# Position product of the first 32 tiles one edge step earlier, into the bank of their logits; ScalarE leaves out steps that do not exist and makes 22 one-hots before its last eviction

## The reference, cut to what matters

```python
agg = segment_sum(x[src], dst); neigh = agg / max(deg, 1)           # 106250 edges
h = x @ W_self + b_self + neigh @ W_neigh
h = prelu(layernorm(h) * gamma + beta) + x ; x1 = x + h              # x is layer-normed on the way in
x2 = layernorm(x1)
logits = x2 @ gate_weight.T ; top_vals, top_idx = top_k(logits, 2)
h = silu(x2 @ w1[e].T) for the picked experts; mean of h over each expert's tokens
y_mean[e] = h_mean[e] @ w2[e].T ; out = x1 + softmax(top_vals) . y_mean[top_idx]
```

## Time and profile before

| | us |
|---|---|
| median of 3 runs | 1636.46 (1634.24 to 1638.45) |
| span of the profiled execution | 1988.1 |
| of it, stretch of the edge steps (about 200 to 1618) | 1418 |
| of it, from 1618 to the end | 370 |
| TensorE, VectorE, GpSimd, ScalarE busy | 1311.0, 1077.1, 967.4, 892.4 |

### The profile page before, as it was taken

The page is one execution under the profiler, slowest core; times in us unless marked ns, Lnnn a source line. Parts: engine busy times, 40 slices in busy tenths (PEclk is TensorE's granted clock), DMA queues, the critical chain, the costliest instruction groups (busy, mean ns, idle before and its releaser), DMA issues.

```text
span 1988.1 us, 36507 instructions
## 1 busy us (share of the span) xinstructions
PE 1311.0 (66%) x7645; PEld 658.9 (33%) x7646; DVE 1077.1 (54%) x2604; ACT 892.4 (45%) x1939; POOL 967.4 (49%) x1237
## 2 busy tenths in 40 slices
PE   5999788995545555455545445455666643999996
PEld 3454344442212222222222222123333322677641
DVE  6663146554545535655655665453453666666626
ACT  3454444445333333333333333233444468888701
POOL 5321656565555556555555655555554511555500
PEclk9999899998778767776777777677778775999986
DMA  6452676766666766676667676665655643666466
GB/s 200 138 163 96 191 222 211 214 207 205 209 200 202 191 192 206 190 232 216 204 214 232 213 220 210 197 183 166 189 172 160 180 172 104 194 201 199 150 242 258
DMA packets 140571, 384.91 MB, mean 194 GB/s; under 512 B 22286, under 2 KB 22416, under 8 KB 140452
## 3 DMA queue, kind: packets, MB, share of 16 engines
q0 software_dynamic: 76416, 250.05, 43.4%
q1 hardware_dynamic: 62392, 130.43, 18.6%
q10 hardware_dynamic: 1644, 3.10, 0.4%
HBM read 323.78 MB, written 59.72 MB: 193 GB/s over the span
## 4 chain that ended last, share of the span: by engine, by line
PE 36%; POOL 22%; issue 19%; DMA 9%; another core or an unknown queue 3%; ACT 3%; DVE 3%; POOLq 3%; DVEq 0%; ACTq 0%; SPq 0%
POOL work L630 22%; PE ps L969 13%; DMA work<-table,work 8%; PE ps L868 8%; PE ps L1062 5%; PE ps L1073 2%; PE ps L1064 2%; POOLq L625 2%; PE ps L1103 1%; ACT slots L780 1%; PE ps L1125 1%; ACT wparts L770 1%; DMA work<-in_x 1%; PE ps L914 1%
## 5 line engine op out<-in xcount | busy, mean ns | idle before, releaser
L630 POOL DMA_INDIRECT work<-table,work x832 | 790.7, 950 | 641.0 <-PE ps L972 263.6
L969 PE MATMUL ps<-work 128*128 x2056 | 667.2, 474 | 544.5 <-DMA work<-table,work 421.2
L969 PEld LDWEIGHTS ps<-work 128*128 128x128 f16 x2056 | 228.7, 113 | 862.1 <-issue 758.1
L723 ACT ACTIVATE work<-work,ones 128x512 f16<-128x512 f16 x259 | 185.4, 716 | 538.0 <-remote 348.7
L717 ACT ACTIVATE work<-iota_row,work 128x128 f16<-128x128 f32 x1040 | 331.3, 390 | 31.6 <-ACT work L723 18.8
L1328 DVE TENSOR_SCALAR inv<-ps 128x1 f32 (+2 forms) x49 | 7.7, 158 | 583.6 <-remote 293.4
L868 PE MATMUL ps<-wparts,slots 128*128 128x512 f16 x1176 | 276.0, 386 | 17.8 <-DVE slots L1246 11.7
L646 POOL DMA_INDIRECT slots<-x_d,betab x114 | 108.0, 947 | 167.0 <-PE ps L1073 85.3
L868 PEld LDWEIGHTS ps<-wparts,slots 128*128 128x128 f16 x1176 | 112.8, 99 | 142.1 <-DVE slots L1246 14.2
L1062 PE MATMUL ps<-work,wparts 128*128 x456 | 155.7, 382 | 3.5 <-ACT wparts L812 2.1
L812 ACT COPY wparts<-ps 128x1024 f16<-128x1024 f16 x114 | 115.3, 1012 | 42.6 <-PE ps L1073 30.1
(11 more groups left out here) (272 smaller groups left out, 1574.0 us busy)
## 6 DMA issues: line engine op xcount, KB each, us to landing
work<-in_x SPq DMA_DIRECT2D x96, 256.0 KB, 2.8
work<-in_w_t SPq DMA_DIRECT2D x48, 512.0 KB, 11.2
work<-table,work POOLq DMA_INDIRECT x832
table<-work SPq DMA_DIRECT2D x48, 256.0 KB, 2.0
x_d<-work SPq DMA_DIRECT2D x48, 256.0 KB
x_d<-slots SPq DMA_DIRECT2D x48, 256.0 KB
out_x<-slots SPq DMA_DIRECT2D x48, 256.0 KB
slots<-x_d SPq DMA_DIRECT2D x41, 256.0 KB
```

The source lines that it names most:

```text
L630: pool.indirect_dma_start(out=gath[:, g % GRING, w, :], out_offset=None, in_=table[:, :], in_offset=bass.IndirectOffsetOnAxis(ap=idx_all[: ...
L723: act.activation(hot[:, slot, :, :], away[:, slot % 2, :, :], ACT.Relu, bias=ones[:, 0:1], scale=-1.0).then_inc(c_hot, 1)
L969: pe.matmul(ps[:, ds(bank, 1), :], hot[:, s, w, :], gath_row[:, ds(at + (2 * w + half) * D, D)].unsqueeze(1), start=False, stop=True, skip ...
```

## The change

1. TensorE: place(0) moves from behind step 255's gate to behind step 254's, and writes bank 6 (`POS_AT`), whose logits of tiles 0 to 31 route(0) has read. Its wait for `d_xt` is dropped.
2. ScalarE: in the late bodies the distances of steps past 256 and the one-hots of steps past 256 are left out (3 x 4 and 2 instructions, with their waits); SyncE's counts fall by 3 and 2.
3. ScalarE: 22 of the 48 pairs, in place of 16, stand before `take_turned(48)`.

```diff
-LOW_FIRST = 16
+LOW_FIRST = 22
-POS_AT = (5, 0)
+POS_AT = (6, 0)
...
-            sp.wait_ge(c_away, STEPS + 3)
-            sp.wait_ge(c_hot, STEPS + 2)
+            sp.wait_ge(c_away, STEPS)
+            sp.wait_ge(c_hot, STEPS)
...
-                    act.wait_ge(c_hot, k + 2)
-                    distance(k + 3, (s + 3) % 2)
-                    one_hots(k + 2, (s + 2) % HOTS)
+                    if not late or k + 3 < STEPS:
+                        act.wait_ge(c_hot, k + 2)
+                        distance(k + 3, (s + 3) % 2)
+                    if not late or k + 2 < STEPS:
+                        one_hots(k + 2, (s + 2) % HOTS)
...
-                    if late and k == STEPS - 2:
-                        pe.wait_ge(d_xt, k - LATE)
+                    if late and k == STEPS - 3:
                         place(0)
```

## The result

The changed kernel took 1630.74 us, median of 8 runs (1629.05 to 1632.73), beside 1634.70 of before on the same chip, also of 8. The ratio is 0.9973 with a 95% interval of 0.9964 to 0.9983: 2.8 to 5.9 us less. One of the 87 timed runs of the kernel before in this study took 2882.5 us and is left out of all ratios and means.

What follows compares the result with a forecast made beforehand. ScalarE's low one-hots were taken as the bound, VectorE 0.2 us behind. Savings of 1.79, 0.82 and 1.31 less 0.1 gave 3.8 us, 4.2 at timed pace; 4.0 taken: 1636.46 to 1632.5 us, range 1629.8 to 1636.5.

Steps and rivals of the forecast that it cites:

- Part 1: ScalarE, ahead of the first low one-hot: leaving out work for steps 258 and 259 saves 1.79 us on the path.
- its remark on 16 pairs: ScalarE before the copy of tile 48: 16 pairs first would leave it idle about 3.1 us there.
- Part 2: TensorE around step 256: place(0) one step earlier, without its wait, ends that step 0.82 us earlier; 1.2 at timed pace.
- the pace: Edge stage in the timed runs: an estimated 4.15 us a step, making the saving 1.2 us instead of 0.82.
- Part 3: ScalarE before the copy of tile 48: 22 pairs first remove its 1.31 us idle time; gate(48) just fits.
- the prediction's own signs: Wrong if gate(48) comes after VectorE asks, route(0) isn't done at place(0), or the list product's end moves without the gather.
- The sum: End of the list product: 3.8 us earlier by the profiled execution, 4.2 by the timed pace; 4.0 taken.
- T: Experiments' theory: VectorE isn't held at rows_to(0) in timed runs; skip and 22 pairs help only together, until VectorE is last.
- Full clock in step 256: TensorE's step 256 may stay at 2.4 GHz, giving 1.45 us more: -5.3, 1631.2 us; chance 0.22.
- VectorE as the bound: List product: if step 256 doesn't move, VectorE still ends at 1672.24, giving -3.0, 1633.5 us; chance 0.15.
- Hidden: Expert stage: another wait, w1's load or an instruction block, holds it, so the time stays 1636.5 us; chance 0.08.
- a stall of ScalarE: Among ScalarE's 22 pairs: a 5.7 us stall ahead of the copy of tile 48 gives 1638.2 us; chance 0.10.

Runs made afterwards that it cites:

- the second trace of before: The kernel before, unchanged, profiled once more for a trace at the pace of the timed runs; one run, 1636.18 us, span 1634.4.
- the run with 1.27: The changed kernel with place(0) back behind step 255, in bank 6 and without its wait; 1630.74 us, ratio 0.9975; VectorE idled 1.27 for place(0).

## Why the prediction came out as it did

**The bound and where the gain arrives: right.** The list product was what moved, ScalarE last before and VectorE a hair behind (0.2 us in both traces of before), and afterwards the last block waits for VectorE. The end of the list product carries through: from there to the end of the span lie 310.4 us before and 310.5 after.

**Part 1, 1.79 on ScalarE: the size right, its place on the path not by itself.** The pairs start 1.8 earlier once the turn of tile 47 takes as long (G + 21.61 against 19.83); the first trace shows 1.4, the turn having taken 1.01 instead of 0.61. Alone it buys nothing, as the run with the skip alone shows: it is worth something only because the 22 pairs take it up. The prediction knew this (its remark on 16 pairs), though it wrote "on the path".

**Part 2, place(0): the step that failed.** The prediction took -0.82 from the profiled execution and -1.2 by the timed pace for VectorE, TensorE's turn and ScalarE. Measured, gnn(48) starts at G + 18.15 before and G + 18.18 after: nothing. The failing term is the pace. I took 4.15 us for a step, a mean over all 257. TensorE's steps in the second trace of before:

```profile
1220.35 1.90 PE L969 MATMUL ps<-work 128*128 x8 [1.17 <-DMA work<-table,work]
...
1259.86 1.90 PE L969 MATMUL ps<-work 128*128 x8 [1.23 <-issue]
```

Ten steps lie between the two starts, 3.95 each. So TensorE was done with ten steps 2.0 earlier than I had it, and place(0) before ended 0.4 ahead of gnn(47) and not 1.4 behind. The idea, that VectorE is late behind route(0) at this pace and goes through without a wait, was right, and it is the very reason why place(0) holds nobody. That it can is shown by the run with 1.27; the estimate there puts it at half a microsecond an execution, against the 0.82 to 1.2 of every execution that were summed.

**Part 3, 22 pairs: right in kind, but they do not just fit.** The prediction had the 22 pairs end 0.9 behind the turn of tile 48 (1636.48 against 1635.56), which gate(48) could bear. They ended 1.65 behind it, and gate(48) came after VectorE asked for it: by the prediction's own signs, the one of being wrong that came true. Two things make up the difference. From the first pair to the end of that turn ScalarE had 12.20 in the first profile and 11.84 in the second one of before. The reason is the turn of tile 47, which in the second profile waits for rows_to(0) and starts 0.11 behind gnn(48); in the first it followed step 256 at once, 0.25 ahead of gnn(48) (1621.05 in the earlier trace rows):

```profile
1620.80 0.61 PE L986 MATMUL ps<-identh,slots 128*128 128x128 f16 x8
```

The other 0.4 is that this turn took 1.01 in the changed kernel's first trace and 0.61 in its second: TensorE had idled 2.48 and 2.06 before it, and the granted clock during it was 0.50 and 1.00. VectorE pays: its last block ends at G + 70.02 against 69.34, later by 0.68 (by 0.26 in the second trace), where the sum had it 0.82 to 1.2 earlier.

**The sum.** Before, the list product ended 73.84 - 69.34 = 4.50 behind VectorE's last block; after, 70.95 - 70.02 = 0.93. That is 3.57 won by taking ScalarE out of the way, less 0.68: 2.89, where 3.8 and 4.2 were summed. 0.51 of the 3.57 is one thing that the sum left out: the last block ran in 0.87, not 1.38. Windows of TensorE (length, busy us and instructions, granted clock, DMA share, GB/s), in the second trace of before around its idle time ahead of the 42, then in the changed kernel over its last three blocks:

```profile
1315.60:1318.90 3.30, 0.17 (x3) 1.00 0.00 0
1319.86:1324.01 4.15, 4.15 (x42) 0.50 0.02 4
```

```profile
1315.66:1319.33 3.67, 2.60 (x42) 1.00 0.02 4
```

In both kernels the clock had risen to 1.00 towards the end of the fourth block. In before it fell back while TensorE idled for ScalarE, and the 42 ran at 0.50; in the changed kernel the three blocks were done before it fell. The waits are part of a burst's price, but not a fixed one: with 16 pairs in the changed kernel the 42 stood behind 4.61 of idle time and took 3.67, as the mean clock over them was 0.59.

**The measured 4.0 us is more than that 2.9**, and the agreement with the forecast is partly luck: an effect that the traces show only in part makes up for the 0.82 to 1.2 that part 2 did not give. The changed kernel was timed twice, each time beside the kernel before on the same chip. By means it took 1630.7 against 1635.4 (8 runs each) and 1629.7 against 1635.4 (7 and 23 runs): 4.7 and 5.7 apart, with standard errors of 0.7 and 0.8, where its two traces show 2.9 and 3.3. For the kernels that T puts within 0.5 us of before, the means, each against before on its own chip, are lower by 0.3 (place(0) alone), 0.5 (the skip alone) and 1.1 (the changed kernel with 16 pairs), with standard errors of 0.5 to 0.6. The slips against which place(0) insures would account for about half a microsecond on the mean, by the estimate above. That they make up the difference was not shown: the run with place(0) behind step 255 was as fast as the changed kernel. So 1 to 2 us of the gain stay open. The stretch behind the list product doesn't hold them, as it took 309.5 to 311.8 us in all 13 traces, 310.4 of it in the kernel before. A single trace can't settle it, since G alone scatters from 1244.8 to 1251.8 over them. Nor was it tried whether the skip and the 22 pairs give all of the gain with place(0) left as it was.

**The rivals.** *Full clock in step 256*: no gain, because step 256 already ran in 1.90 in the kernel before at this pace; the 3.35 of the earlier trace rows belonged to the slower profiled execution. The granted clock did cost TensorE time elsewhere, at the list product: 42 matmuls took 4.15 behind 4.09 idle, at a clock of 0.50, and 0.87 a block (2.61 for 42) behind 0.2 to 1.1 idle, at 1.00. The Trainium skill, TensorE: Matmul & The Clock Gate, section on a second HAM failure mode, has short idle times between groups of matmuls swing the clock. At this pace the trace doesn't agree: behind place(0)'s idle times of 0.82 and 1.33 step 256 had a granted clock of 1.00, and between the blocks, with 0.15 to 1.06 idle, the clock rose and did not fall. *VectorE as the bound*: this is what happened, at -2.9 by the traces, beside its -3.0, though by another road: it lost 0.68 to gate(48), which no step of that rival had. *Hidden* and *a stall of ScalarE*: neither was seen.

## What to carry to other kernels

When two engines end within 0.2 us of each other, work saved on one is worth only what the other lets through, and two parts that give nothing alone can be worth 1.6 more beside one that gives 1.3 alone (by the traces): read each part by the next wait it runs into (here the turn of tile 48), not by its length. Before taking a wait from a profile whose span is far from the timed runs, take the pace of the stretch in question and not a mean over the stage; a wait with 0.4 us of slack turns either way. A freed wait elsewhere (turn_x2(47)'s for `i_row`, once the bank had moved) is worth looking for right after such a change.

## What the runs showed of the hardware

GpSimd and VectorE were not free of each other. A GpSimd tensor_scalar of 128x128 f16 took 0.78 to 0.85 us (up to 1.13 beside VectorE's instructions) against 0.23 on VectorE, and one that met VectorE's run of 12.19 us of tensor_tensor blocks (two inputs in SBUF) took 12.96: nothing got through in between. The other way round, 40 of them cost VectorE 1.1 us over route(1) and what follows it up to the blocks. The Trainium skill, SBUF — State Buffer, section "SBUF: two separate sides", calls the pair of ports that the two share an exclusive lock held for the whole of one instruction. The trace agrees that the two block each other, and shows more: seven back-to-back VectorE instructions let no GpSimd instruction in between them.

The profiled execution of an unchanged kernel can differ by a fifth: 1988.1 us in one, 1634.4 in another, with 641.0 us of idle time of GpSimd ahead of its gathers in the first page and 291.0 in the second. The timed runs, with a median of 1634.6 beside that second trace, are of its kind.
